# Turned one-hots of a graph kernel: made once and kept in DRAM instead of made in every attention pass

## What is computed

```python
# L2, three layers (the kernel's "gin" passes)
msg = relu(h_in[src] + edge_attr @ conv_edge_w[l] + conv_edge_b[l])
agg = segment_sum(msg, dst)
# ... two dense layers on h_in + agg, and a virtual node

# L3, three layers (the kernel's "gat" passes), 4, 4 and 1 heads
m = xl[src] + xr[dst] + ea @ We
s = einsum('ehc,hc->eh', leaky_relu(m, 0.2), att)
ex = exp(s - segment_max(s, dst)[dst])
out = segment_sum(xl[src] * (ex / segment_sum(ex, dst)[dst])[:, :, None], dst)
```

## Time and profile before

| what | us |
|---|---|
| three runs | 9355.59, 9361.79, 9379.95 |
| median | 9361.79 |
| the profiled execution | 9320.16 |
| its span, first to last instruction | 9318.2 |
| gathers of the three gin passes, first to last start | 2317.6 to 3303.4, 3352.8 to 4338.5, 4387.4 to 5373.2 |
| gathers of the three gat passes | 5442.1 to 6651.8, 6727.7 to 7947.4, 8026.4 to 9221.2 |

### The profile page before, as it was taken

One profiled execution on the slowest core, in us unless ns is written; L12 is line 12 of the kernel. 1 busy time (PEld: TensorE's weight loads), 2 busy tenths in 40 slices (PEclk: granted clock), 3 DMA queues, 4 the chain that ended last, 5 costly groups with the idle time before them and its releaser, 6 DMA issues. The chain is left out here.

```text
span 9318.2 us, 197548 instructions
## 1 busy us (share of the span) xinstructions
PE 7645.8 (82%) x49731; PEld 5556.8 (60%) x49914; DVE 5974.4 (64%) x15460; ACT 3792.3 (41%) x10443; POOL 5148.8 (55%) x5386
## 2 busy tenths in 40 slices
PE   4999999988666666666666689999899999899997
PEld 1443344887444434444444467888688788688886
DVE  6999999022333333333333368888878788778888
ACT  2222222301111111111111156777666677667776
POOL 0000000000777767776777758878577787577774
PEclk9999999999677776777677779999889899899998
DMA  1000011854222222222222212222122222122221
GB/s 43 7 21 26 30 42 42 342 217 165 59 60 60 61 55 60 60 60 56 59 60 60 61 49 59 59 56 58 48 57 58 55 58 57 47 59 57 56 57 42
DMA packets 372820, 615.17 MB, mean 66 GB/s; under 512 B 114410, under 2 KB 277569, under 8 KB 355988
## 3 DMA queue, kind: packets, MB, share of 16 engines
q0 software_dynamic: 150528, 308.58, 12.7%
q1 hardware_dynamic: 221460, 296.64, 9.2%
HBM read 509.70 MB, written 94.96 MB: 65 GB/s over the span
## 5 line engine op out<-in xcount | busy, mean ns | idle before, releaser
L535 POOL DMA_INDIRECT rows_and_onehots<-node_table,idx x4704 | 4978.7, 1058 | 1367.8 <-issue 1185.3
L762 PEld LDWEIGHTS ps<-rows_and_onehots,w 128*128 128x128 f32 x5280 | 1029.2, 282 | 1717.7 <-issue 1675.8
L762 PE MATMUL ps<-rows_and_onehots,w 128*128 128x128 f32 x5280 | 1098.6, 376 | 1085.8 <-issue 1050.3
L530 POOL COPY idx<-src_g 128x8 int32 (+1 forms) x594 | 152.5, 257 | 2642.3 <-DMA node_table<-hr 2549.3
L1219 DVE TENSOR_TENSOR w<-rows_and_onehots,ps 128x512 f32<-128x512 f32 x663 | 456.2, 688 | 1726.9 <-POOLq L546 1361.8
L656 ACT ACTIVATE w<-w 128x512 f32<-128x512 f32 x663 | 417.3, 629 | 2589.0 <-DVE w L1219 2589.0
L859 PE MATMUL ps<-w_L_conv_edge,ea 65*128 65x512 f32 x1326 | 974.1, 828 | 31.7 <-DMA ea<-in_ea 26.1
L712 ACT ACTIVATE hr<-iota_d,dloc 128x128 f32<-128x128 f32 x2724 | 871.0, 390 | 2.1 <-issue 1.3
L908 PE MATMUL ps<-w_L_gnn_We,hr 128*128 128x512 f32 x1344 | 824.7, 698 | 33.8 <-issue 30.0
L912 PEld LDWEIGHTS ps<-xrb,hr 128*128 128x128 bf16 x8064 | 569.3, 106 | 450.2 <-issue 450.2
L613 ACT ACTIVATE xrb<-iota_d,local_dst 128x128 f32<-128x128 f32 x976 | 298.7, 389 | 1085.5 <-DVE local_dst L1133 1085.5
(11 more groups left out here) (240 smaller groups left out, 12650.0 us busy)
## 6 DMA issues: line engine op xcount, KB each, us to landing
rows_and_onehots<-node_table,idx POOLq DMA_INDIRECT x4704
hr<-in_ea SPq DMA_DIRECT2D x672, 64.0 KB
w<-adjacency_turned SPq DMA_DIRECT2D x26, 1600.0 KB, 6.9
adjacency<-rows_and_onehots SPq DMA_DIRECT2D x25, 1600.0 KB, 5.2
w<-adjacency SPq DMA_DIRECT2D x25, 1600.0 KB, 12.0
rows_and_onehots<-adjacency_turned SPq DMA_DIRECT2D x24, 1600.0 KB, 7.1
adjacency_turned<-rows_and_onehots SPq DMA_DIRECT2D x17, 1600.0 KB, 7.8
ea<-in_ea SPq DMA_DIRECT2D x672, 32.0 KB
```

The source lines that it names most:

```text
L535: pool.indirect_dma_start(out=G[q][:, (i % CH) * D:(i % CH + 1) * D], out_offset=None, in_=table[:, :], in_offset=bass.IndirectOffsetOnAxi ...
L762: m = pe.matmul(bank(u % 2, P), rows[u][:, c * D:(c + 1) * D], OH[u][:, c * P:(c + 1) * P], start=(c == 0), stop=(c == CH - 1))
```

## The change

In the first gin pass, after each scatter, PE turns the float32 one-hot of that step with four float32 transposes into PSUM bank 4 or 5. ACT copies the bank out twice, as float32 and as bf16, into two staging tiles each, and SP stores both into two new tables in DRAM (256 KB and 128 KB a step). The gat passes no longer have the bf16 relu, the transposes and the two copies. SP instead loads both turned one-hots of each step, after the attributes. `OHTB` has four buffers where it had two, and the loads of a gat step now wait for projection and scan of step s-4 where they waited for step s-8. SP also waits for the start of the edge pass on the other engines before its first load, since the loads now write over tiles that the dense work before it uses. PE waits for the one-hot ahead of the segment maxima (it used to wait ahead of the transposes). At the end of the first gin pass ACT waits until all stores have landed, and DVE until all copies are done.

```diff
-        OHB = [sb(f"OHB{i}", [P, CH * P], BF16) for i in range(2)]
-        OHTB = [hr[:, 2592 + i * 256:2592 + (i + 1) * 256].bitcast(BF16) for i in range(2)]
+        OHTB = ([hr[:, 2592 + i * 256:2592 + (i + 1) * 256].bitcast(BF16) for i in range(2)]
+                + [sb(f"OHTB{i}", [P, CH * P], BF16)[:, :] for i in (2, 3)])
+        turned32 = spare[RING:RING + 2]
+        turned16 = [spare[RING + 2][:, i * 256:(i + 1) * 256].bitcast(BF16) for i in range(2)]
-        turned = bank(0, CH * P // 2).bitcast(BF16)
+        onehots32 = nc.dram_tensor("turned_onehots_f32", (NSG * P, CH * P), F32, kind="Internal").ap()
+        onehots16 = nc.dram_tensor("turned_onehots_bf16", (NSG * P, CH * P), BF16, kind="Internal").ap()
...
+            def store_turned(s, u):
+                row = s * P if isinstance(s, int) else sp.snap(s * P)
+                held(sp, onehots_copied, s + 1)
+                for to, staged in ((onehots32, turned32), (onehots16, turned16)):
+                    sp.dma_start(to[bass.ds(row, P), :], staged[u % 2]).then_inc(onehots_stored[u % 2], 16)
...
                     held(sp, S["projected"], s - depth + 1)
                     if "scanned" in S:
-                        held(sp, S["scanned"], s - RING + 1)
-                    parts(g, u)
+                        held(sp, S["scanned"], s - depth + 1)
+                    parts(g, u, s)
+                    if then:
+                        then(s, u)
...
+                def turned_parts(s, u):
+                    if not isinstance(s, int) or s >= 6:
+                        store_turned(s - 6, u - 6)
+                edge_rows(GIN[l], f"gin {l} edges", 4, gin_parts, turned_parts if l == 0 else None)
+                if l == 0:
+                    for s in range(NSG - 6, STEPS):
+                        store_turned(s, s)
+                    for s in range(STEPS, NSG):
+                        for to, staged in ((onehots32, turned32), (onehots16, turned16)):
+                            sp.dma_start(to[s * P:(s + 1) * P, :], staged[0]).then_inc(onehots_stored[0], 16)
...
+                begin(sp, f"gat {l} edges")
+                if l == 0:
+                    for i in range(2):
+                        sp.wait_ge(onehots_stored[i], ALL_STORED[i])
...
-                edge_rows(GAT[l], f"gat {l} edges", RING, gat_parts)
+                    for of, to in ((onehots16, OHTB[u % 4]), (onehots32, OHT[u])):
+                        sp.dma_start(to, of[bass.ds(s * P, P), :]).then_inc(GAT[l]["edge_data"][u], 16)
+                edge_rows(GAT[l], f"gat {l} edges", 4, gat_parts)
...
+                def copy_turned(s, u):
+                    act.wait_ge(onehots_turned, s + 1)
+                    held(act, onehots_stored[u % 2], (s - u % 2) * 16)
+                    act.copy(turned32[u % 2], bank(4 + u % 2))
+                    act.copy(turned16[u % 2], bank(4 + u % 2)).then_inc(onehots_copied, 1)
+                if l == 0:
+                    copy_turned(STEPS - 1, STEPS - 1)
+                    for i in range(2):
+                        act.wait_ge(onehots_stored[i], ALL_STORED[i])
...
-                    if on(s + 5):
-                        act.wait_ge(S["turned"], s + 6)
-                        act.copy(OHT[(u + 5) % RING], turned)
-                        held(act, S["projected"], s + 4)
-                        act.copy(OHTB[(u + 1) % 2], turned).then_inc(S["onehot_t"], 1)
-                    act.activation(OHB[(u + AHEAD) % 2][:, :], far, ACT.Relu, scale=-1.0, bias=1.0)
...
+                    if turns:
+                        held(pe, onehots_copied, s - 1)
+                        for c in range(CH):
+                            m = pe.transpose(bank(4 + u % 2)[:, c * P:(c + 1) * P], OH[u][:, c * P:(c + 1) * P], ident[:, :])
+                        m.then_inc(onehots_turned, 1)
...
-                    pe.wait_ge(S["onehot_t"], s + 1)
-                    if on(s + 5):
-                        pe.wait_ge(S["onehot"], s + 6)
-                        held(pe, S["onehot_t"], s + 5)
-                        for c in range(CH):
-                            m = pe.transpose(turned[:, c * P:(c + 1) * P], OHB[(u + 1) % 2][:, c * P:(c + 1) * P],
-                                             identb[:, :])
-                        m.then_inc(S["turned"], 1)
+                        pe.wait_ge(S["onehot"], s + 3)
...
+                if l == 0:
+                    dve.wait_ge(onehots_copied, STEPS)
```

More of the change, by code:

```diff
@@ L288, in build @@
         summed_up, sums_out = sem("summed_up"), sem("sums_out")
+        onehots_turned, onehots_copied = sem("onehots_turned"), sem("onehots_copied")
+        onehots_stored = [sem(f"onehots_stored{i}") for i in range(2)]
+        ALL_STORED = [32 * (STEPS // 2 + NSG - STEPS), 32 * (STEPS // 2)]
         PARTS = BANKS + 1
@@ L312, in build @@
         GIN = [sems(f"gin {l} edges", "projected", "summed", "rectified", rows=1) for l in range(3)]
-        GAT = [sems(f"gat {l} edges", "turned", "onehot_t", "projected", "summed", "leaky", "attended", "score",
+        GAT = [sems(f"gat {l} edges", "projected", "summed", "leaky", "attended", "score",
                     "score_t", "scanned", "scan_back", "seg_rhs", "seg_max", "seg_out", "chunk_max", "step_max",
                     "new_max", "max_drop", "kept",
-                    "far", "scale", "max_of_edge", "delta", "fall", "weight", "weighted", "rescaled", rows=2)
+                    "far", "scale", "max_of_edge", "delta", "fall", "weight", "weighted", "rescaled", rows=4)
                for l in range(3)]
@@ L402, in store, with edge_rows @@
                                  x[:, c:c + w].rearrange("p (t f) -> p t f", f=D)).then_inc(stored, 16)
-            def edge_rows(S, l_at, depth, parts):
+            def store_turned(s, u):
[3 more added lines that the diff above has]
+                    sp.dma_start(to[bass.ds(row, P), :], staged[u % 2]).then_inc(onehots_stored[u % 2], 16)
+            def edge_rows(S, l_at, depth, parts, then=None):
                 sp.wait_ge(stored, IN_TABLE[l_at])
@@ L656, in rectify, with body @@
                     act.activation(rows[u], rows[u], ACT.Relu).then_inc(S["rectified"], 1)
-                rectify(0, 0)
-                walk(act, lambda s, u, r=rectify: r(s + 1, (u + 1) % RING), rounds=13)
+                def copy_turned(s, u):
[3 more added lines that the diff above has]
+                    act.copy(turned16[u % 2], bank(4 + u % 2)).then_inc(onehots_copied, 1)
+                def body(s, u, rectify=rectify, copies=l == 0):
+                    rectify(s + 1, (u + 1) % RING)
+                    if copies and on(s - 1):
+                        copy_turned(s - 1, u - 1)
+                rectify(0, 0)
+                walk(act, body, rounds=13)
+                if l == 0:
+                    copy_turned(STEPS - 1, STEPS - 1)
+                    for i in range(2):
+                        act.wait_ge(onehots_stored[i], ALL_STORED[i])
                 if l < 2:
@@ L862, in _, with body @@
                 project(0, 0)
-                def body(s, u, S=S, project=project):
+                def body(s, u, S=S, project=project, turns=l == 0):
                     project(s + 1, (u + 1) % RING)
@@ L908, in project @@
                     pe.matmul(term[u % 2], ea4[u], W[f"L3_gnn_We{l}"][:, :], start=True, stop=False)
-                    pe.wait_ge(S["onehot_t"], s + 1)
                     for c in range(CH):
                         for k in range(3):
-                            m = pe.matmul(term[u % 2][:, c * D:(c + 1) * D], OHTB[u % 2][:, c * P:(c + 1) * P],
+                            m = pe.matmul(term[u % 2][:, c * D:(c + 1) * D], OHTB[u % 4][:, c * P:(c + 1) * P],
                                           right[k], start=False, stop=(c == CH - 1 and k == 2))
@@ L1417, in _ @@
                 take_sums(STEPS - 1, (STEPS - 1) % RING)
-                for k, more in (("projected", 4), ("turned", 5), ("onehot_t", 5), ("onehot", AHEAD), ("seg_out", 2),
+                for k, more in (("projected", 4), ("onehot", AHEAD), ("seg_out", 2),
                                 ("score_t", 3), ("scan_back", 2)):
```

7 lines of the change are left out of this document (2 added, 5 removed).

## The result

| | before | after |
|---|---|---|
| median of 20 runs each, us | 9351.68 | 9397.49 |
| the profiled execution, span | 9318.2 | 9371.4 |
| mean granted clock of the profiled execution | 0.862 | 0.857 |

The ratio is 1.0043, with a 95% interval of 1.0032 to 1.0054: slower by 0.43%, where the prediction said 0.37% faster. The time lies inside the range given.

The account below looks back on a forecast made before the run. Gin was taken as POOL-bound, a gat pass as a balance of nearly saturated POOL, DVE's 4.91 us floor and PE at low clock. -45 + 10 = -35 us took 9361.8 to 9327 us; range 9225 to 9455.

Parts of the forecast that it names:

- The gin gathers: First gin pass: POOL-bound, so the added PE, ACT and SP work costs 0 us; gathers still 986 us first to last.
- the tail: End of first gin pass: last transposes and copies 1.9 us, ten stores 4.5, landing some 3; +10 us once, bounds 5 and 20.
- loads and gathers in time: Gat loads need some 6 of 11.2 us; gin gathers have 1.6 us of room beside the stores; both cost 0.
- DVE's running step: Gat passes: DVE's fifteen operations a step form a floor that stays at 4.91 us, 1080 us a pass.
- Rival 2: Gat passes: PE was the bound, so its removed transposes pay in full, -191 + 10 us; time 9181; chance 0.12.
- rival 1: Gat passes: nothing comes back, as POOL and DVE trade waits and DVE waits for POOL instead; time 9372; chance 0.20.
- Rival 4: First gin pass: gathers land late beside the stores and POOL waits, 127 us more; time 9454; chance 0.08.
- the term of -45 us: Gat passes: with less PE work, half of the 89.8 us that POOL waits for used groups comes back.
- rival 3: Gat passes: PE no longer fills running steps, the granted clock falls and the kernel is slower, +76 us; time 9448; chance 0.12.
- one stretch of 52 us at clock 1.00: Gat passes: PE was busy 50.55 of 52 us at full clock, so not every gap makes the clock fall.
- The slope from the earlier trace: Gat step: 5.48 us at clock 0.92, 7.1 at 0.78, so 0.02 of clock costs 0.23 us a step, 152 us, half shadowed.
- on no path: Gat passes: ACT, busy 874 of 1212 us, loses a relu and two copies; worth nothing except at the start of a pass.

Follow-up runs that it names:

- four fillers: Changed kernel plus four bf16 transposes of a constant identity, read by nobody, on TensorE in each gat step: ratio 1.0015 to the kernel before, median 9356.52 us.
- the kernel before with the loads: Kernel before plus two loads (256 KB and 128 KB) in each gat step into unread tiles, ring of loads four deep, PE's work unchanged: ratio 1.0036.
- two fillers: Changed kernel plus two unread bf16 transposes of a constant identity in each gat step, run twice: 1.0085 (beside an unusually slow kernel before) and 1.0039 (likewise).

## Why the prediction was wrong, point by point

**Right.** The gin gathers (986 us), the clock apart; the tail, +10 forecast and +9.8 measured, with some luck (ten issues took 6.1 us and not 4.5, the landing 2.7 and not 3, and that leaves 1.0 for the transposes and copies where the sum had 1.9); loads and gathers in time, no wait of POOL for landed gathers above 0.3 us, nor of PE for loads but at the starts of the passes; DVE's running step, still 4.91 (L1429 starts at 6929.80 and 6934.71). Rival 2 (PE as the plain bound, 9181) is refuted. So is rival 1's reason: DVE waited less for POOL, not more. Rival 4 (the gathers of the first gin pass 127 us longer) didn't come.

**The step that failed** is the term of -45 us, "half" of POOL's 89.8 us of waiting. It took PE's lag as a debt that a shorter PE step pays off sooner, at a clock that stays. The clock didn't stay. POOL's wait for used groups went to 147.6, not to 45. It was rival 3, to which I gave 0.12: its condition, a gat clock of 0.90 or less, was met with 0.88. My argument against it was one stretch of 52 us at clock 1.00, picked for that clock; it can't tell how often running steps lose it. The count above does: low stretches that began without a pause of PE of 0.6 us went from 41 to 86, and with four fillers back to 40. Rival 3's own words, that PE no longer fills running steps, fit that. What in a running step makes the clock fall the runs don't show.

**The price was wrong as well.** Rival 3 had 76 us for 0.02 of clock, 38 for 0.01. The clock fell by 0.04, and the kernel lost 46 - 10 = 36 us outside the tail, 9 for 0.01. The four fillers give the same: 26 us for 0.023 (0.88 to 0.903), 11 for 0.01. Both are net prices. PE's work changed along with the clock, by up to 191 us off or back on, and rival 3 had counted nothing for the shorter work; what the clock alone costs at equal work no run shows. The slope from the earlier trace rows also compared a stretch with stalls in it and one without: of its 19 us, PE stood still in 8.05 - 1.45 = 6.6. With the net price and the measured clock the forecast would have been 9361.8 + 10 + 36 = 9408; that is no test of the price, since 36 us is read from the result.

**A term was missing.** The gat passes grew by 37 us from first to last gather, and what lies between and behind them by 11 us in the profile. The sum had nothing for the latter.

**ACT was counted as on no path.** The forecast gave nothing for taking work off it. Whether that is right isn't shown: the changed kernel with four fillers (1.0015) and the kernel before with the loads (1.0036) have the same count of matmuls a step and the same KB, and differ in ACT's work among other things, but their intervals overlap. The move of one small operation to it (1.0573) shows how close ACT was to the path.

**Open**: what in a running step lowers the clock, and whether a delay of 0.29 us would do what the fillers do; why 384 KB of loads a step cost the kernel before 0.36% (0.19 to 0.54), and whether they cost the changed one anything; what a dose of two fillers gives; and whether DVE's 4.91 us is a floor that pays.

## What to carry to other kernels

When work leaves TensorE in a stage whose length other engines set, put the granted clock of the stage after the change into the forecast as its own term: fewer matmuls can mean a lower clock and a later PE. Read its price from two versions of a kernel with and without filler work, not from two stretches of one trace at different clocks, since the one at the lower clock holds stalls of its own; what is read so is the net of the clock and of PE's work, which is what such an edit pays. And price an operation by the distance from the start before it to the start behind it, with and without it, not by its duration.

## What the runs showed of the hardware

- Four bf16 transposes a step of a constant, read by nobody, raised the granted clock of the gat passes from 0.88 to 0.90-0.91 and took 26 us off (1.0043 to 1.0015); eight raised it to 0.93 and took nothing off (1.0044).
- Low stretches of the clock began without a pause of PE of 0.6 us or more in the two steps before: 41 of 83 before the change, 86 of 116 after it, 40 of 86 with four fillers, 10 of 47 with eight. In one place PE was busy 29.95 of 30 us before the clock fell.
- Over the 29 runs of the kernel before that stood beside the fillers, time and mean granted clock go together: 0.001 of clock over the whole kernel for 6.6 us (correlation -0.87). That doesn't say which sets which.
- In one place a DVE operation of 0.16 us between two others cost 0.01 us: 0.19 us from start to start with it, 0.18 without.
